# Layer-norm normalisation moved from VectorE to GpSimd, and the residual step cut into three stages, in a one-core attention and expert block

## The reference

```python
h = layernorm(x) * (1 + ca) + sa
x = x + ga * attention(h)            # 16 heads of 8, causal, rotary, 1024 keys
h = layernorm(x) * (1 + cb) + sb
x = x + gb * ffn(h)                  # router picks 1 of 8 experts of 64, h = leaky(h)**2
```

## Time and profile before

| what | value |
|---|---|
| median of 3 runs | 417.24 us (416.14 to 418.75) |
| the profiled execution | 420.04 us, its span 418.3 us |
| PE busy | 365.2 us (87%) |
| DVE busy | 259.9 us (62%) |
| ACT busy | 219.1 us (52%) |
| POOL busy | 101.3 us (24%) |
| mean granted PE clock | 0.931 of full |

### The profile page before, as it was taken

One profiled execution on the slowest core, in us unless ns is written; L12 is line 12 of the kernel. 1 busy time (PEld: TensorE's weight loads), 2 busy tenths in 40 slices (PEclk: granted clock), 3 DMA queues, 4 the chain that ended last, 5 costly groups with the idle time before them and its releaser, 6 DMA issues.

```text
span 418.3 us, 6846 instructions
## 1 busy us (share of the span) xinstructions
PE 365.2 (87%) x2350; PEld 170.3 (41%) x2383; DVE 259.9 (62%) x566; ACT 219.1 (52%) x415; POOL 101.3 (24%) x185
## 2 busy tenths in 40 slices
PE   6948855989689799896999998999999999999876
PEld 3424521534454245332333343444334445434545
DVE  3546771768766656773677777667787777313144
ACT  5231332645216625563566665656676766685333
POOL 3302562336400023231022210200303222213110
PEclk9978995999858988996799999999999999999989
DMA  7374272001100000162304040000000000000000
GB/s 258 108 204 98 94 186 51 2 3 56 44 6 0 0 2 27 64 120 48 98 1 114 3 107 8 2 2 25 3 0 3 4 1 4 3 1 2 25 2 25
DMA packets 12337, 18.86 MB, mean 45 GB/s; under 512 B 3600, under 2 KB 8592, under 8 KB 12176
## 3 DMA queue, kind: packets, MB, share of 16 engines
q1 hardware_dynamic: 12016, 18.04, 16.0%
q10 hardware_dynamic: 288, 0.39, 0.3%
HBM read 12.98 MB, written 5.24 MB: 44 GB/s over the span
## 4 chain that ended last, share of the span: by engine, by line
PE 72%; DVE 6%; issue 6%; DMA 5%; ACT 4%; SPq 4%; POOL 3%; ACTq 0%; POOLq 0%; DVEq 0%
PE ps_o L963 16%; PE ps_a L925 15%; PE ps_b L943 15%; PE ps_a L902 3%; PE ps_s L831 3%; PE ps_s L895 3%; PE ps_s L882 3%; DMA qst<-negt 2%; SPq L388 2%; DVE tmax L780 2%; PE ps_a L920 2%; ACT pt L601 2%; PE ps_s L849 2%; DVE rot L692 1%; PE ps_s L863 1%
## 5 line engine op out<-in xcount | busy, mean ns | idle before, releaser
L780 DVE TENSOR_REDUCE tmax<-ps_a 128x1 f32<-128x512 f32 (+3 forms) x304 | 187.9, 656 | 98.9 <-PE ps_a L925 98.4
L601 ACT ACTIVATE pt<-ps_b 128x512 f32<-128x512 f32 (+1 forms) x304 | 166.0, 574 | 130.5 <-PE ps_b L943 128.6
L943 PE MATMUL ps_b<-qst,kst 75*128 75x512 bf16 (+3 forms) x384 | 117.9, 341 | 15.2 <-DMA qst<-negt 10.8
L925 PE MATMUL ps_a<-kst,qst 72*128 72x128 bf16 (+3 forms) x576 | 119.5, 288 | 5.8 <-issue 2.7
L963 PE MATMUL ps_o<-pt,v_sb 128*32 128x512 f32 (+3 forms) x768 | 84.3, 513 | 0.4 <-POOL pt L497 0.3
L925 PEld LDWEIGHTS ps_a<-kst,qst 72*128 72x128 bf16 x576 | 52.1, 103 | 71.2 <-DVE tmax L780 37.6
L497 POOL TENSOR_SCALAR_AFFINE_SELECT pt<-pt 128x512 f32<-128x512 f32 x64 | 40.1, 636 | 85.7 <-ACT pt L601 85.4
L943 PEld LDWEIGHTS ps_b<-qst,kst 75*128 75x128 bf16 x384 | 35.3, 100 | 47.3 <-ACT pt L601 22.2
L468 POOL CAST negp<-negm 128x16 bf16<-128x16 f32 x16 | 3.1, 196 | 114.5 <-DVE negm L713 114.4
L902 PE MATMUL ps_a<-maska,identb 128*128 128x512 bf16 x89 | 27.2, 400 | 3.4 <-POOL maska L434 3.3
L963 PEld LDWEIGHTS ps_o<-pt,v_sb 128*32 128x32 f32 x768 | 15.5, 110 | 31.5 <-issue 19.9
(11 more groups left out here) (107 smaller groups left out, 307.8 us busy)
## 6 DMA issues: line engine op xcount, KB each, us to landing
qst<-qparts SPq DMA_DIRECT2D x48, 96.0 KB
kst<-kparts SPq DMA_DIRECT2D x48, 96.0 KB
qparts<-part SPq DMA_DIRECT2D x4, 384.0 KB, 2.6
kparts<-part SPq DMA_DIRECT2D x4, 384.0 KB, 2.7
xs<-in_x SPq DMA_DIRECT2D x4, 256.0 KB, 7.1
rope_sb<-in_rope SPq DMA_DIRECT2D x1, 1024.0 KB, 7.0
qparts<-part SPq DMA_DIRECT2D x4, 256.0 KB, 2.9
qst<-negt SPq DMA_DIRECT2D x48, 4.0 KB, 1.7
```

What stands on the lines that cost most here:

```text
L601: act.activation(pt[:, G % NP, h0:h0 + nh, 0:w], src, ACT.Exp, scale=SCALE).then_inc(s_exp, 1)
L780: dve.tensor_reduce(dst, src, AX.X, ALU.max).then_inc(s_max, 1)
L925: last = pe.matmul(dst[:, j * nk:(j + 1) * nk], qst[0:ROWS, half, h, r * P:r * P + P], kst[0:ROWS, kh, h, k0:k0 + nk], start=(kind != "dia ...
L943: last = pe.matmul(ps_b[:, n % 2, j * w:(j + 1) * w], kst[:, kh, h, kt * P:kt * P + P], qst[:, half, h, c0:HALF], start=True, stop=True)
```

## The change

Three things are changed:

- The normalisations of three preps, (0,1), (1,0) and (1,1), and of three posts, (0,0), (0,1) and (1,1), are computed by POOL (24 of the 32 instructions of L663). POOL waits for its own `rstd` and runs them in the stage `nz` or `ln`. The first prep and the last unit's two pieces stay on DVE.
- Statistics and aggregates are separate stages. In a prep, `norm1` keeps the `bn_stats`, and `var1` one distance later has the `bn_aggr`, `veps` and `rstd`. In a post, `out` keeps only the residual sum, `st` one slot later has the `bn_stats`, `var2` one slot after that the `bn_aggr`, `veps` and `rstd`.
- The tables follow: `ln` stays three slots behind `out`; in a prep, `nz` was 3 slots behind `norm1` (2 + 1) and is now 4 behind it (1 + 1, twice), so that every later stage of the preps (1,0) and (1,1) is one slot later.

```diff
-PREP = {"norm1": 0, "nz": 2, "hT": 3, ...
-POST = {"oT": 2, "out": 2, "ln": 3, "h2": 3, ...
+PREP = {"norm1": 0, "var1": 1, "nz": 1, "hT": 3, ...
+POST = {"oT": 2, "out": 2, "st": 1, "var2": 1, "ln": 1, "h2": 3, ...
...
+        def on_pool(u):
+            return u != PREPS[0] and u[0:2] != UNITS[-1] or len(u) == 2 and u == UNITS[-1]
+
+        def normalise(eng, dst, src, t0, t1):
+            for t in range(t0, t1):
+                last = eng.tensor_scalar(dst[:, t], src[:, t], mv[:, t, 0:1], rstd[:, t:t + 1],
+                                         ALU.subtract, ALU.mult)
+            last.then_inc(s_xn, 1)
...
 # POOL
             def rstd_of(st):
-                t0, t1 = (0, TU) if st[0] == "norm1" else tiles(st[1])
-                pool.wait_ge(s_var, nth(st, "norm1", "out") + 1)
+                t0, t1 = (0, TU) if st[0] == "var1" else tiles(st[1])
+                n = nth(st, "var1", "var2")
+                pool.wait_ge(s_var, n + 1)
                 pool.tensor_tensor(rstd[:, t0:t1], veps[:, t0:t1], mhalf[:, t0:t1], ALU.pow).then_inc(s_rstd, 1)
+                if on_pool(st[1]):
+                    pool.wait_ge(s_rstd, n + 1)
...
-                if name in ("norm1", "out"):
+                if name in ("var1", "var2"):
                     rstd_of(st)
+                if name == "nz" and on_pool(u):
+                    if prep_no[u]:
+                        wait_read(pool, "hT", PREPS[prep_no[u] - 1])
+                    normalise(pool, xn, xs[:, 2 * u[0] + u[1]], 0, TU)
+                if name == "ln" and on_pool(u):
+                    if unit_no[u[0:2]]:
+                        wait_read(pool, "h2", last_piece(unit_no[u[0:2]] - 1))
+                    normalise(pool, xn2, x2, *tiles(u))
...
 # DVE
                 for t in range(t0, t1):
                     last = dve.bn_stats(stats[:, t], src[:, t])
-                link(last)
+                count[0] += 1
+                last.then_inc(s_dve, 1)
+
+            def aggregate(t0=0, t1=TU):
+                dve.wait_ge(s_dve, count[0])
                 for t in range(t0, t1):
                     last = dve.bn_aggr(mv[:, t], stats[:, t])
                 link(last)
                 dve.tensor_scalar(veps[:, t0:t1], mv[:, t0:t1, 1], EPS, None, ALU.add).then_inc(s_var, 1)
...
+                if name == "var1":
+                    aggregate()
+                if name == "nz" and not on_pool(u):
+                    modulation_columns()
+                    dve.wait_ge(s_rstd, nth(("var1", u), "var1", "var2") + 1)
+                    normalise(dve, xn, xs[:, 2 * u[0] + u[1]], 0, TU)
...
+                if name == "st":
                     wait_read(dve, "out", u)
                     statistics(x2, nth(st, "nz", "ln"), t0, t1)
-                if name == "ln":
-                    normalise(xn2, x2, nth(("out", u), "norm1", "out"), t0, t1)
+                if name == "var2":
+                    aggregate(t0, t1)
+                if name == "ln" and not on_pool(u):
+                    dve.wait_ge(s_rstd, nth(("var2", u), "var1", "var2") + 1)
+                    normalise(dve, xn2, x2, t0, t1)
```

More of the change, by code:

```diff
@@ L91 @@
             **{f"m{c}": 1 for c in range(4)}}
-PREP = {"norm1": 0, "nz": 2, "hT": 3, "q1": 3, "q2": 3, "q3": 3, "k1": 3, "k2": 3, "k3": 3, "v": 5}
-POST = {"oT": 2, "out": 2, "ln": 3, "h2": 3, "rt": 2, "a0": 2, "a1": 2, "ohT": 2, "a2": 2, "a3": 2, "m0": 2, "m1": 2,
+PREP = {"norm1": 0, "var1": 1, "nz": 1, "hT": 3, "q1": 3, "q2": 3, "q3": 3, "k1": 3, "k2": 3, "k3": 3, "v": 5}
+POST = {"oT": 2, "out": 2, "st": 1, "var2": 1, "ln": 1, "h2": 3, "rt": 2, "a0": 2, "a1": 2, "ohT": 2, "a2": 2, "a3": 2, "m0": 2, "m1": 2,
         "m2": 2, "y0": 1, "m3": 3, "y1": 4}
-POST_LAST = ["oT", "out", "ln", "h2", "rt", "a0", "a1", "ohT", "m0", "a2", "m1", "a3", "m2", "y0", "m3", "y1"]
+POST_LAST = ["oT", "out", "st", "var2", "ln", "h2", "rt", "a0", "a1", "ohT", "m0", "a2", "m1", "a3", "m2", "y0", "m3", "y1"]
 PREP_AT = [[0, 0], [40, 1], [86, 1]]
@@ L106 @@
 HIDDEN = ("a0", "a1", "a2", "a3")
-PRE = [("mod", 0)] + [(name, (0, 0)) for name in ["norm1", "nz", "hT", "q1", "k1", "q2", "q3", "k2", "k3", "v"]] \
-    + [("load", (0, 0), g) for g in range(NG)] + [(name, (0, 1)) for name in ["norm1", "nz", "hT"]]
+PRE = [("mod", 0)] + [(name, (0, 0)) for name in ["norm1", "var1", "nz", "hT", "q1", "k1", "q2", "q3", "k2", "k3", "v"]] \
+    + [("load", (0, 0), g) for g in range(NG)] + [(name, (0, 1)) for name in ["norm1", "var1", "nz", "hT"]]
 def plan():
@@ L658, in statistics @@
                 dve.tensor_scalar(veps[:, t0:t1], mv[:, t0:t1, 1], EPS, None, ALU.add).then_inc(s_var, 1)
[L660 to L665, removed]
             def run(st):
```

## The result

| | before | after |
|---|---|---|
| median (runs) | 418.0 us (4, 416.14 to 419.6) | 434.29 us (4, 428.94 to 436.39) |
| the profiled execution | 420.04 us | 433.81 us |
| its span, mean granted PE clock | 418.3 us, 0.931 | 432.1 us, 0.912 |

The ratio is 1.035 (95% interval 1.024 to 1.046): slower, outside the forecast range. A second comparison, beside the experiments, gave 433.28 us and 1.043 (1.036 to 1.050). In the experiments the kernel before ran at a median of 415.8 us on the two chips that took all but the last of them (13 runs on one, 11 and 16 on the other), and at 417.6 on the third (7 runs).

A forecast was written before the change was run, and what follows sets the result against it. TensorE, with 72% of the chain, was taken to bound the kernel. Costs of 1.1 + 1.2 + 0.75 + 0.1 + 0.25 = 3.4 us on the 417.24 us median gave 420.6 us, range 414 to 426.5.

The forecast's parts named there:

- the price: Each normalisation instruction on POOL was to take 0.35 us, four of them 1.4 us (1.2 to 1.8).
- POOL is dear: Slower rival: four POOL normalisations take 3.6 us, 2.2 us more in four places; 429.4 us, chance 0.1.
- Post (0,0): Slots 72 to 80: PE's 2.33 us wait goes, `v` falls behind the transposes, about 3 us idle; cost 1.1 us.
- Post (0,1): Slots 196 to 202: PE's 0.75 us wait becomes 1.75 us; transposes 1.2 us later (0.95 to 1.6).
- Post (1,1): Slots 304 to 310: rstd moves behind slot 305's zeroing, ending a 0.32 us PE wait; cost 0.75 us (0.5 to 1.15).
- Prep (1,0): Slots 41 to 49: a 0.74 us PE wait goes, but POOL's chain ends later; +0.1 us (-0.3 to +0.4).
- Prep (1,1): Free: later aggregates and POOL's extra 0.4 us fit into 2.6 us between ready tiles and transposes.
- Prep (0,1): Before slot 0: tiles 0.4 to 0.8 us later, hidden behind a 2.05 us wait for the keys' DMA.
- Tail: Last two pieces interleave on DVE, making POOL's two rstd back to back; cost 0.25 us (-0.1 to +0.7).
- The latency is hidden: Rival: the norm is ready when PE comes, so only relief from old waits remains; 415.7 us, chance 0.15.
- The clock does not fall: Faster rival: slot 73's early maximum keeps PE fed and removes a half-clock stretch, 6.3 us; 414.3 us, chance 0.15.
- The clock falls once more: Slower rival: the pause at slot 201 brings another half-clock stretch, 5.3 us more; 425.9 us, chance 0.2.

The follow-up runs named there:

- the kernel with filler: The changed kernel with PE multiplying a constant during five waits for POOL ahead of transposes, no wait shortened: 426.61 us, ratio 1.024.
- the split alone: The changed kernel with all normalisations back on DVE, keeping the separate stages and shifted slots: 415.23 us, ratio 0.996 against before.
- POOL's cheaper form: The changed kernel with POOL's 24 instructions using two fixed numbers instead of each token's mean and rstd: 423.91 us, ratio 1.022.
- the norms twice: The changed kernel with the three posts' normalisations on POOL computed twice, first into an unused tile: 449.94 us, ratio 1.075.
- the split without the slip: All normalisations on DVE, stages separate, but the preps' `nz` back at three slots behind `norm1`: 420.89 us, ratio 1.015.
- the move alone: The kernel before with the same 24 normalisations on POOL, no stages separated and no slot shifted: 429.23 us, ratio 1.031.
- the posts alone: The changed kernel with only the three posts' normalisations on POOL and the preps' on DVE: 426.22 us, ratio 1.028.

## Why the prediction was wrong

**The step that failed** is the price: "I take 0.35 us, 1.4 us for four (1.2 to 1.8)". It was 0.79 and 3.13 us. I had reasoned from the number of tensor inputs, and set the new instruction between POOL's select with one input and its multiplication with two. Since the same instruction has a mean of 0.36 us on DVE in the earlier trace rows, this took POOL to be as fast as DVE. The form matters more: two fixed numbers in place of the pointers still take 0.645 us, more than the two-input instruction on the same tile. The Trainium skill, "GPSIMD Engine Reference", section 4.1, gives elementwise work on a tile to VectorE, and the runs agree (1.11 us for four against 3.13). The same section of the Trainium skill puts one-input work on GpSimd roughly at line rate, and this case's traces disagree: 0.645 to 0.79 us for one on POOL, 0.34 in the median for one on DVE.

With the measured price in it, my sum would have been 1.7 us larger in the three posts and in prep (1,0), 6.8 us in all: 430.2 against the profiled execution's 433.81, and 427.4 against the median's 434.29, which is already outside the range. That this comes near is partly luck: the sum would have 10.2 us for the waits alone, where the kernel with filler puts them at about 6.6, and nothing for the half-clock time, which grew by 17.6 us from the first profile of before to that of after. The rival "POOL is dear" had nearly this price (3.6 us) and gave 429.4 for it, at a chance of 0.1.

**The second** is that the clock stood among the rivals, as one fall more or less with "10.7 us of PE work", and not in each term of the sum. Each pause was priced at its own length. In the first profile after, PE's pauses of 1.6 us (prep (1,0)), 3.2 (post (0,1)) and 1.8 (post (1,1)) are followed by 11, 8 and 7 us at half clock; in the second, the first two by 11 and 11, and the third by none. Filler in the pauses, with the waits left, gave 6.7 us back.

**Point by point.**

- Post (0,0): places and order right. The 2.33 us became 0.80 + 0.75, not nothing; `v` runs at 130.58, behind the transposes; the pause is 4.27 us where I had 3; with the price's 1.7 it would be 4.7.
- Post (0,1): 3.17 us for 1.75 forecast. The difference of 1.4 is within the 1.7 by which the price was too low.
- Post (1,1): right in its order. The zeroings run ahead of rstd at 363.45, and the product (PE, L986, at 366.25) has no wait. The pause is 1.79.
- Prep (1,0): "I take +0.1 us" failed. The transposes wait 1.56 us, about the 1.7 by which the price was too low, and half-clock time follows in both profiles.
- Prep (1,1): free, as said. POOL's last started at 151.8 and ended at 152.6, 1.7 us ahead of the transposes at 154.26, the dear price included.
- Prep (0,1): the cover held for all but about 0.5 us, even at the dear price. The wait ahead of its transposes grew from 3.56 to 5.57 us, and the first pass A bank, at 31.10, no longer waits for the keys' DMA. It looks 2.65 us late against the earlier trace rows, but 2.2 us of that lie at the start, which is slower in this execution: eight multiplications of filler take 3.57 us there and 1.89 in the first profile of before, though the view of windows gives a clock of 1.00 in both. The second profile of before has the slower start too, and its bank stands 0.46 us ahead of that of after:

```profile
30.64 0.61 PE L920 MATMUL ps_a<-maska,identb 128*128 128x512 bf16 x1 [1.57 <-DMA kst<-kparts]
```

- Tail: the two rstd stand back to back, as said:

```profile
411.91 1.40 POOL L464 TENSOR_TENSOR rstd<-veps,mhalf 128x2 f32<-128x2 f32 x2 [6.73 <-DVE veps L685]
```

- DVE's busy time fell by 7.1 us (6.6 forecast), none of it on the path, and the kernel with the split alone, which has the early maxima and the slip, gains nothing measurable.

**The rivals.** "The latency is hidden" fell at all places but one. "The clock does not fall" fell: 124 to 142 stands at 0.53 after. "The clock falls once more" happened, and more than once: behind prep (1,0) and post (0,1) in both profiles, behind post (1,1) in one. Longer pauses went with more half-clock time (58.0 us with POOL's cheaper form, 75.6 and 88.8 after, 102.4 with the norms twice). The two slow rivals were not alternatives, as I had weighed them: the one brings the other.

## What to carry to other kernels

An instruction that no row shows should be priced by its form and operands on that engine, not by its number of inputs; where its latency lies ahead of the bounding engine, it is the first thing to measure by itself, and until then the range must hold the dear case. A pause of TensorE is to be priced with the stretch behind it: in the two experiments that changed only POOL's time, a microsecond of waiting went with 1.4 to 3. That is no fixed rate: the split alone has 3.3 us more waiting than before and the same time, and the split without the slip has less waiting and more time. An estimate from the 12 profiled executions without added filler, by a linear fit of their spans to half-clock time and waits ahead of transposes, is about 0.4 us of span for a microsecond at half clock and 0.6 for one of waiting. And an engine that is busy for 28% of the span is not free, if its work stands between two steps of one chain.

## What the runs showed of the hardware

- POOL's `tensor_scalar` with two operations on 128 x 128 float32: 0.79 us with scalars per token, 0.645 with fixed numbers. DVE takes 0.34 in the median for the form with scalars per token, 0.36 on the mean of the shape in the kernel before; four in a row take 3.13 us on POOL and 1.11 on DVE.
- Behind pauses of PE of 1.6 to 3.2 us the granted clock stood near one half for 7 to 11 us in the first profile of after, though PE was busy for nearly all of it (370 to 377: 7.00 us of 7.00; 90 to 101: 10.38 of 11). Around the pause of 4.27 us it did so from 124 to 142.
- A pause alone doesn't decide it. At prep (1,0) a fall came with each pause of 1.5 to 2.1 us, in five profiled executions of four kernels, and none with a pause of 0.4 to 0.9 us, in seven of six. At post (1,1) a pause of 1.8 to 1.9 us had a fall behind it in two executions (after, the move alone) and none in two others (after again, the posts alone). The 1.52 us that made one at prep (1,0) were a wait for DVE.
- The falls vary from execution to execution of one kernel (47.8 and 58.0 us; 75.6 and 88.8), while the waits ahead of transposes repeat (18.4 us twice).
- The start's filler takes 1.89 us for eight multiplications in one execution of the kernel before and 3.57 in the other; the first pass A bank came 2.2 us later in the latter.
- POOL beside DVE cost DVE's maxima nothing that can be seen: their mean is 658 ns after and 656 before.
